# Shorter durations for TensorE in the planner that orders a four-layer attention kernel

## What is computed

```python
# layer 0, 16 heads, q/k/v and attention weights rounded to 8 bits
x = attn_q(ln(x), ln(x)) + x            # a1: self-attention
x = attn_q(ln(x), ctx) + x              # a2: cross-attention
a, g = split(ln(x) @ ff_w1); x = a * gelu(g) @ ff_w2 + x       # geglu
# layer 1, 16 heads, rmsnorm
x = attn(rms(x), rms(x)) + x            # sa
x = attn(rms(x), ctx) + x               # ca
x = silu(rms(x) @ wg) * (rms(x) @ wu) @ wd + x                 # swiglu
# layer 2, 8 heads
x = x + mha(ln(x), ln(ctx))             # mh
U = (ln(x) @ W_in.T + b_in) @ Bmat      # drive
s = silu(s @ A.T) + u_t                 # recurrence over 256 steps
x = x + states @ Cmat + mod
# layer 3: attention to ctx, softmax over the queries, then a layernorm
```

## Time and profile before

| what | us |
|---|---|
| median of the timed runs | 3099.52 (3098.40 to 3101.69) |
| the profiled execution, its time | 3103.99 |
| its span, first to last instruction | 3102.2 |
| TensorE busy in the span | 2496.9 (80%) |
| VectorE busy | 1807.0 (58%) |
| ScalarE busy | 1360.5 (44%) |
| GpSimd busy | 880.6 (28%) |
| mean granted clock of TensorE | 0.843 of full |

### The profile page before, as it was taken

How to read it: one execution, slowest core, us unless ns; L and a number is a source line. 1 busy time by engine, 2 the same in 40 slices (tenths; PEclk the granted TensorE clock), 3 DMA queues, 4 the chain that set the end, 5 groups by cost and what they waited for, 6 DMA issues and landing times. The chain is left out here.

```text
span 3102.2 us, 47313 instructions
## 1 busy us (share of the span) xinstructions
PE 2496.9 (80%) x16568; PEld 1807.3 (58%) x16568; DVE 1807.0 (58%) x4271; ACT 1360.5 (44%) x3566; POOL 880.6 (28%) x1096
## 2 busy tenths in 40 slices
PE   4359997989888889888989798989789765448997
PEld 3247675757566757565867576666567443334443
DVE  3965657674666675767576856666753320005766
ACT  3535446353444453535454544535442311224554
POOL 3540223322232231332232312222320010005766
PEclk9669997889798989787989898879798765558999
DMA  5320101210020111111111101111110010001110
GB/s 189 57 48 3 24 12 34 42 27 15 21 39 20 25 34 22 30 30 26 26 29 23 37 17 29 23 28 23 35 22 4 5 36 5 0 0 34 36 37 22
DMA packets 222407, 90.45 MB, mean 29 GB/s; under 512 B 205280, under 2 KB 212784, under 8 KB 221424
## 3 DMA queue, kind: packets, MB, share of 16 engines
q1 hardware_dynamic: 215728, 67.68, 11.2%
q10 hardware_dynamic: 6464, 19.93, 1.7%
HBM read 27.80 MB, written 9.44 MB: 12 GB/s over the span
## 5 line engine op out<-in xcount | busy, mean ns | idle before, releaser
L1037 PE MATMUL psum<-hT,w_l 128*128 128x256 f32 x2048 | 496.0, 402 | 14.5 <-ACT hT L1364 12.0
L1037 PEld LDWEIGHTS psum<-hT,w_l 128*128 128x128 f32 x2048 | 410.1, 203 | 87.4 <-issue 13.5
L757 POOL TENSOR_TENSOR rstd<-ms,half 128x2 f32<-128x2 f32 (+1 forms) x144 | 101.7, 706 | 953.7 <-DVE ms L1121 614.0
L1488 ACT ACTIVATE work<-psum,nbias,qs 128x256 f32<-128x256 f32 x512 | 281.9, 566 | 117.9 <-DVE nbias L1200 117.5
L1504 ACT ACTIVATE work<-psum 128x1024 f32<-128x1024 f32 (+1 forms) x224 | 221.2, 1022 | 242.7 <-PE psum L969 172.7
L862 PE MATMUL psum<-hT,w_l 128*128 128x256 f32 x896 | 241.7, 422 | 22.2 <-ACT hT L1364 20.0
L797 POOL TENSOR_SCALAR work<-work 128x1024 f32<-128x1024 f32 x128 | 136.9, 1070 | 366.5 <-DVE work L1294 332.5
L1049 PE MATMUL psum<-w_l,work 128*128 128x256 f32 x1024 | 228.2, 381 | 4.2 <-DVE work L1317 2.3
L862 PEld LDWEIGHTS psum<-hT,w_l 128*128 128x128 f32 x896 | 184.6, 213 | 64.4 <-ACT hT L1364 18.5
L871 PE MATMUL psum<-w_l,xhat 128*128 128x256 f32 x640 | 189.6, 449 | 38.9 <-DVE xhat L1273 27.3
L1197 DVE TENSOR_REDUCE nmax<-psum 128x4 f32<-128x1024 f32 (+1 forms) x192 | 206.2, 1074 | 17.5 <-PE psum L917 16.8
(11 more groups left out here) (185 smaller groups left out, 4840.4 us busy)
## 6 DMA issues: line engine op xcount, KB each, us to landing
w_l<-in_w_l ACTq DMA_DIRECT2D x1, 5120.0 KB, 25.6
x_res<-in_x SPq DMA_DIRECT2D x16, 256.0 KB, 2.6
res<-x_res ACTq DMA_DIRECT2D x16, 256.0 KB, 2.3
w_l<-res SPq DMA_DIRECT2D x16, 256.0 KB, 2.8
out<-w_l ACTq DMA_DIRECT2D x16, 256.0 KB, 2.0
w_l<-in_w_l ACTq DMA_DIRECT2D x1, 3072.0 KB, 13.9
work<-work SPq DMA_TRANSPOSE x192, 3.1
w_l<-in_w_l SPq DMA_DIRECT2D x2, 1024.0 KB, 8.5
```

The lines of the kernel that those rows point to most:

```text
L1037: mm = eng.matmul(banks.tile(key)[:, h * TOKENS:(h + 1) * TOKENS], w1[:, k, h, m * P:(m + 1) * P], hT[p][:, k, :], start=(k == 0), stop=(k ...
L1488: ins = eng.activation(e[:, h * TOKENS:(h + 1) * TOKENS], s[:, h, :], ACT.Exp, bias=nbias[:, r, h:h + 1], scale=qs[:, ATTENTIONS.index(a), ...
```

## The change

Only durations of TensorE's tasks in `plan()` change. The core of the diff:

```diff
-        x = work.add("tensor", "norm", name, 0, p, 0.55, x, used,
+        x = work.add("tensor", "norm", name, 0, p, 0.45, x, used,
...
-                s = work.add("tensor", "scores", a, (u, i), p, 0.5, q, k, rounds.get(2 * u + i - HELD),
+                s = work.add("tensor", "scores", a, (u, i), p, 0.25 if a.self_attn else 0.15, q, k, rounds.get(2 * u + i - HELD),
...
-                    s = work.add("tensor", "scores_t", a, (half, kt, i), p, 0.85 if a.halves == 2 else 2.1, t,
+                    s = work.add("tensor", "scores_t", a, (half, kt, i), p, {SA: 0.85, CA: 0.5, MH: 1.4}[a], t,
...
-            f = work.add("tensor", "hidden", name, m, p, 1.85, hT, fills=[(("f", name, m, p), 1, ("vector", "hidden", name, m, p))])
+            f = work.add("tensor", "hidden", name, m, p, 1.75, hT, fills=[(("f", name, m, p), 1, ("vector", "hidden", name, m, p))])
```

More of the change, by code:

```diff
@@ L197, in out @@
     def out(a, p, bias, *o):
-        y = work.add("tensor", "out", a, 0, p, 1.85, *o, fills=[(("y", a.name, p), 1, ("vector", "residual", a.name, 0, p))])
+        y = work.add("tensor", "out", a, 0, p, 1.75, *o, fills=[(("y", a.name, p), 1, ("vector", "residual", a.name, 0, p))])
         return work.add("vector", "residual", a.name, 0, p, 0.7, y, bias)
     def project(a, p, hT, reader, what, us, *before):
-        full = work.add("tensor", what, a, 0, p, 1.85, hT,
+        full = work.add("tensor", what, a, 0, p, 1.75, hT,
                         fills=[((what[0], a.name, p), 1, ("scalar" if a.quant else reader, what, a, 0, p))])
@@ L241, in quantised @@
             if qt or not a.self_attn:
-                weighed = work.add("tensor", "weigh", a, ft, p, 0.9 if a.self_attn else 0.5, *evacuated, v,
+                weighed = work.add("tensor", "weigh", a, ft, p, 0.5 if a.self_attn else 0.25, *evacuated, v,
                                    fills=[(("o", a.name, ft, p), 1, ("scalar", "outputs", a, ft, p))])
@@ L261, in soft @@
                 if part[0] == half:
-                    s = work.add("tensor", "scores", a, part, p, 0.85 if a.self_attn else 0.75, q, k,
+                    s = work.add("tensor", "scores", a, part, p, 0.7 if a.self_attn else 0.75, q, k,
                                  fills=[(("s", a.name, part, p), 2, ("vector", "maxima", a, part, p))])
                     m.append(work.add("vector", "maxima", a, part, p, 1.25 if a.self_attn else 1.0, s))
-            t = work.add("tensor", "turn_max", a, half, p, 0.5 if a.halves == 2 else 1.0, *m,
+            t = work.add("tensor", "turn_max", a, half, p, 0.3 if a.halves == 2 else 0.5, *m,
                          fills=[(("t", a.name, half, p), 1, ("vector", "shift", a, half, p))])
@@ L276, in soft @@
                 for ft in [half] if a.halves == 2 else range(KT):
-                    weighed[ft, kt] = work.add("tensor", "weigh", a, (ft, kt), p, 1.3, *e, v,
+                    weighed[ft, kt] = work.add("tensor", "weigh", a, (ft, kt), p, 0.95, *e, v,
                                                weighed.get((ft, kt - 1)),
@@ L286, in mlp @@
         for m in range(MT):
-            f = work.add("tensor", "hidden", name, m, p, 1.85, hT, fills=[(("f", name, m, p), 1, ("vector", "hidden", name, m, p))])
+            f = work.add("tensor", "hidden", name, m, p, 1.75, hT, fills=[(("f", name, m, p), 1, ("vector", "hidden", name, m, p))])
             g = work.add("scalar", "hidden", name, m, p, 0.5, f, acts[m - 4] if m >= 4 else None)
             acts.append(work.add("vector", "hidden", name, m, p, 0.45 if name == "geglu" else 1.0, g, *acts[-1:]))
-        y = work.add("tensor", "down", name, 0, p, 7.4, acts[-1], fills=[(("y", name, p), 1, ("vector", "residual", name, 0, p))])
+        y = work.add("tensor", "down", name, 0, p, 7.0, acts[-1], fills=[(("y", name, p), 1, ("vector", "residual", name, 0, p))])
         return work.add("vector", "residual", name, 0, p, 0.7, y, bias)
@@ L332, in plan @@
         c = work.add("vector", "normalise", "lnc", 0, p, 0.4, c)
-        c = work.add("tensor", "norm", "lnc", 0, p, 0.3, c, *used, fills=[(("lnc", p), 1, ("scalar", "norm", "lnc", 0, p))])
+        c = work.add("tensor", "norm", "lnc", 0, p, 0.2, c, *used, fills=[(("lnc", p), 1, ("scalar", "norm", "lnc", 0, p))])
         context_of(MH, p, work.add("scalar", "norm", "lnc", 0, p, 0.6, c))
```

## The result

The changed kernel takes 3189.66 us (3186.25 to 3194.61), the one before 3098.96 us in the same session; the ratio is 1.0292, with a 95% interval of 1.0274 to 1.0310. That is 90.7 us more, where 29 us were forecast.

A forecast was written before the change was run, and what follows sets the result against it. TensorE was taken as the bound (88% busy in the steady part). A period of 150.75 us, the middle of two estimates, against 148.3 gave 2.4 us times twelve, 29 us: 3128 us, range over all cases 3045 to 3190.

The forecast's parts named there:

- the correction of the old stretch: Old period between `mlp_n` cuts of batches 4 and 5, 159.3 us, less extra pieces 2.4, `ln3` wait 2.2, `keys` wait 3.6: 151.1.
- The second estimate: Old stretch from batch 5 to 6, also 105 pieces, 145.4 us, plus the 5.04 us pause at `sa_n`: 150.4 us.
- GpSimd "at nothing": GpSimd, busy 404.7 of 1483.2 us, keeps its work; its cost was priced at nothing, its idle rest as cover.
- Are the new durations truer?: Planner's table: truer at full clock, not after a pause (eight projection matmuls 1.99 or 3.78 us); said not to move the sum.
- The pause at `sa_n`: Transposes of `sa_n` still wait 3 to 5.5 us each period, as VectorE's residual stands behind two sets of `probs`.
- Banks: PSUM banks that move make pieces wait for other readers: 16 us either way, taken as 0.
- table loads: ScalarE's planned loads rise from 42 to 64, 28 us on that engine; already counted in the 151.1 us.
- Head and tail: First two batches and after batch 14: few pieces change place, taken as 0, plus or minus 8 us.
- Rival (2): The pause spreads: lower clock after `sa_n` and loads pushing `a1` give 156.9 us a period, some 3200 us; chance 0.12.
- Rival (1): Even spacing pays: steady periods settle at 142 to 146 us, 3024 to 3072 us, some 3050; chance 0.32.

The follow-up runs named there:

- Experiment 1: Changed kernel with VectorE and GpSimd lists edited so the second half of `a2`'s probabilities goes ahead of other work, batches 4 to 13: 3158.9 us, ratio 1.0201.
- kernel 14: Changed kernel's table with cross-attention's `weigh` at 1.9 us, its transposed scores at 1.0, out-projections of cross-attention and `a2` at 3.7: 3069.9 us, ratio 0.9912.
- 17: Kernel before, its own table, with cross-attention's `weigh` at 1.9 us and the out-projections of cross-attention and `a2` at 3.7: 3068.6 us, ratio 0.9909.
- 15: Kernel before with one number changed, `weigh` of the three softmax attentions 0.95 us in place of 1.3: 3082.3 us, ratio 0.9941.
- kernel 13: Changed kernel's table with cross-attention's `weigh` at 1.9 us and its transposed scores at 1.0 us: 3134.2 us, ratio 1.0106.
- experiment 4: Changed kernel's lists kept, PSUM banks as the old durations give them (288 of 1648 tiles elsewhere): 3197.1 us, ratio 1.0320.
- experiment 10: Changed kernel with `hidden.geglu.7` ahead of memory attention's first transposed scores and their exponentials, 44 table loads in place of 64: 3182.7 us, ratio 1.0295.
- experiment 9: Changed kernel, lists and banks untouched, with 12 matmuls of no use ahead of each transpose of `sa_n`: 3165.6 us, ratio 1.0227.
- Experiment 12: Changed kernel with list edits for `a2`, `sa_n`, out-projections and table loads together, plus eight matmuls of no use ahead of `sa_n`: 3180.0 us, ratio 1.0278.
- 6: Kernel before with only the new, short durations of `scores`, `scores_t`, `turn_max` and `weigh`: 3147.8 us, ratio 1.0167.
- 16: Kernel before, lists and banks unchanged, with 5 to 13 matmuls of no use in each of its eleven longest norm pauses: 3096.0 us, ratio 0.9995.
- 18: On kernel 14, seven matmuls of no use ahead of the transposes of `mlp_n` in batches 6 to 13: 3091.5 us, ratio 0.9987.

## Why the prediction was wrong

The direction was right and the size was not: +2.4 us a period were forecast for twelve periods, and +8.2 came on the mean of ten (156.5 against 148.3), 82 of the 90.7 us. The remaining 8 us are scatter between executions: the two profiled ones differ by 82.3. The time lies at the very end of the range.

**The step that failed is the correction of the old stretch** (159.3 less 8.2 is 151.1), which lets every wait that it does not name stay as it was. What was taken off was right: the transposes of `ln3` have no wait, no projection of `a1` waits more than 1.0 us, and TensorE is busy 132.3 us in the new period against 134.55 - 2.4 = 132.15. But idle time is 24.7 us, the 24.75 of the old stretch unchanged. The 5.8 us of pauses that went were paid again: 5.1 us at `weigh` of `a2`, which did not wait in the old stretch, and 0.7 us more at `sa_n` (5.75 for 5.04). 151.1 + 5.1 + 0.7 is 156.9, and 157.0 was measured. That this comes out to 0.1 us is in part chance. Two more waits of the old stretch went, which the prediction does not name:

```profile
930.96 1.05 PE L989 MATMUL psum<-work,vpad 128*32 128x256 bf16 x16 [1.52 <-DMA work<-work]
...
1014.72 1.12 PE L853 MATMUL psum<-ident,xhat 128*128 128x128 f32 x4 [3.29 <-ACT xhat L1379]
```

These 4.8 us, at a `weigh` of `a1` and ahead of `mlp_n`, came back in the shorter waits of the new period (each at most 2.7 us; 13.9 us together against 8.9). I asked what each pause was hidden by in the new order and not what had been hidden in the old one: I never compared the lists of VectorE and GpSimd around `weigh` of `a2`. Experiment 1 shows that this one chain was worth 31 us.

The second estimate (150.4) fell short by 6.5 us, and half of that is the clock: its stretch has the same 105 pieces and 128.9 us of busy time, and the new period is busy 132.3 us, with 51.2 us at the lower clock against 32.8 there. The sum had no term for that.

**GpSimd "at nothing"** failed with it. Its idle share (28% busy) is no cover for a task that stands behind a MEMSET which waits for TensorE.

**"Are the new durations truer?"** named the right mechanism and waved it off: pieces behind a pause last twice what the new table says, "it would not move my sum, since the stretch priced holds its share of slow matmuls". It holds slow matmuls, but an order built without them puts urgent work behind them. Experiments 14 and 17 speak for the other side: with lower-clock durations for three or four pieces either table gives a kernel 0.9% faster than before. They don't show that it is the truth of the numbers that pays: 15, with one number made less true, is 0.6% faster, and 13, with two of the three true numbers, 1.1% slower.

**The pause at `sa_n`** stayed, for the reason given (the residual behind two `probs`) and one more, ScalarE's exponentials ahead of `normalise`. It was to be 3 to 5.5 us and was 5.75. **Banks** at 0 (experiment 4) and **table loads** at 0 (64 of them, as computed; experiment 10) were right. The Trainium skill (ScalarE: Activation LUTs, "What ACT_TABLE_LOAD costs") gives 2.66 us for each switch, by which, as an estimate, the end would have come up to 30 us later still. The trace agrees with its 1.28 us for the load and shows no drain. **Head and tail** at 0 was right (711.6 against 711.3 us ahead of the ten stretches, 907.5 against 907.7 behind them).

**Rival (2)** had the number, 156.9 a period and 3200 us, and half of the cause: after the pause TensorE does fall to the lower clock, and experiment 9 prices that at 24 us. Its other half, loads that push the chain of `a1`, experiment 10 does not bear out. Rival (1) was wrong on the change. That an even order can run at its 142 to 146 us is shown by kernel 14 (143.4), another even order; kernel 13, nearly the same lists, ran at 153.5.

**Open.** What decides in which of its periods a repeating order settles. Experiment 12 shows 150.7 and 157.0 from the same lists, 13 and 14 show 153.5 and 143.4 from nearly the same. Until that is known, kernel 14's gain over the changed one (120 us) is half less idle time (about 7 us a period) and half clock, and I can't say that either half is a property of its three numbers; for the clock, not even that it is one of the order rather than of where the run happened to settle. Of the change's 91 us experiment 1 gives back 31 and experiment 9 gives back 24; no run shows that the two add, and for the rest there are only the waits in the trace.

## What to carry to other kernels

When a pause is to go, look for what was hidden behind it: compare the lists of all engines ahead of each waiting piece, since a task that a list puts behind a late one waits for it on whatever engine. Be wary of giving a list planner durations read at full clock for pieces that run at the lower one: here such a table cost 2.9%, and lower-clock durations for a few pieces gave 0.9% on two tables, though a falser number gave 0.6% on one, so try several tables and measure. Judge such a change by many periods and by busy time apart from idle time: two kernels whose lists and banks differ little differed by 10 us a period, nearly all of it matmuls at the lower clock.

## What the runs showed of the hardware

Evenly repeated work can settle at more than one period. The same 934 matmuls took 153.6, then 150.7 and then four times 157.0 us in one run (12), at a granted clock of 0.87, 0.90 and 0.86. Experiments 1 and 6, and 9 for five periods, run at 153.6 us though they change different things. A fill in a pause paid 24 us where the clock was at full and fell in the pause (9), nothing in irregular pauses (16), and cost 22 us where the clock was still down when it came (18). Of `ACT_TABLE_LOAD`, 20 fewer at 1.28 us each made no measurable difference on an engine that is 44% busy (10).
